# Two-layer decoder kernel: the first layer's scatters issued one step later, and its last group's router weights computed earlier

## The reference, cut to what matters

```python
x = x + linear_attention(norm(x))            # first layer
x = x + cross_attention(norm(x), ctx_1024)   # 16 heads, softmax over 77 keys
x = x + experts(norm(x))                     # 16 experts, two per token, capacity 640
x = x + latent_attention(norm(x))            # second layer
x = x + cross_attention_1head(norm(x), ctx_1024)
x = x + quantised_ffn(norm(x))
```

```python
top_vals, sel = top_k(sigmoid(xf @ gate_w.T), 2)
weights = top_vals / (top_vals.sum(-1, keepdims=True) + 1e-06)
slot = where(rank < 640, expert * 640 + rank, none)   # rank: place of the token in its expert's queue
padded[slot] = x                                      # each token is written to two slots
out = (expert_output[slot] * weights).sum(axis=1)
```

## Time and profile before

| | us |
|---|---|
| median of 3 runs | 1657.05 |
| lowest and highest of them | 1647.87, 1658.19 |
| the profiled execution, its own time | 1666.73 |
| its span in the trace | 1664.7 |

### The profile page before, as it was taken

How to read it: one execution, slowest core, us unless ns; L and a number is a source line. 1 busy time by engine, 2 the same in 40 slices (tenths; PEclk the granted TensorE clock), 3 DMA queues, 4 the chain that set the end, 5 groups by cost and what they waited for, 6 DMA issues and landing times. The chain is left out here.

```text
span 1664.7 us, 26844 instructions
## 1 busy us (share of the span) xinstructions
PE 1514.0 (91%) x9735; PEld 1071.9 (64%) x9735; DVE 1014.5 (61%) x2312; ACT 900.2 (54%) x2289; POOL 473.1 (28%) x625
## 2 busy tenths in 40 slices
PE   8999999898977889999999899999999989996299
PEld 5766777676656767787777566666666654442288
DVE  3657878888886335222222566766664568777883
ACT  4457786675786222211212555666656633597980
POOL 3212334344345300000002665555533300032100
PEclk9999999999997899999999999999999979998599
DMA  4441111111241144333424211110100000000031
GB/s 120 153 160 25 39 38 40 37 51 51 82 133 45 58 154 136 123 114 125 152 90 137 71 39 52 41 35 28 39 14 14 1 26 1 0 0 18 21 101 64
DMA packets 105281, 109.33 MB, mean 66 GB/s; under 512 B 29762, under 2 KB 94156, under 8 KB 105152
## 3 DMA queue, kind: packets, MB, share of 16 engines
q1 hardware_dynamic: 99008, 91.06, 17.8%
q0 software_dynamic: 6144, 16.57, 3.1%
HBM read 65.81 MB, written 42.01 MB: 65 GB/s over the span
## 5 line engine op out<-in xcount | busy, mean ns | idle before, releaser
L2121 ACT ACTIVATE c_pr<-bank,c_nmax 128x256 f32<-128x256 f32 x256 | 117.7, 472 | 118.0 <-DVE c_nmax L2238 117.9
L1827 POOL TENSOR_SCALAR c_pr<-c_pr,c_rsum 128x256 f32<-128x256 f32 x256 | 127.6, 514 | 186.4 <-DVE c_rsum L2243 186.0
L1558 ACT ACTIVATE b_G<-bank 128x320 f32<-128x320 f32 x128 | 55.9, 437 | 210.4 <-PE bank L1507 210.4
L1507 PE MATMUL bank<-b_XT,shared 128*128 128x320 f32 x512 | 154.2, 436 | 0.0
L2238 DVE TENSOR_REDUCE c_nmax<-bank 128x2 f32<-128x512 f32 x128 | 82.4, 686 | 105.8 <-PE bank L1886 102.5
L1521 PE MATMUL bank<-shared,b_G 128*128 128x256 f32 x640 | 142.2, 379 | 0.0
L959 ACT ACTIVATE a_L<-a_L,a_Lm 128x77 f32<-128x77 f32 x512 | 131.2, 353 | 4.4 <-DVE a_Lm L1097 4.3
L1521 PEld LDWEIGHTS bank<-shared,b_G 128*128 128x128 f32 x640 | 120.9, 190 | 17.8
L508 POOL TENSOR_TENSOR a_Pm<-a_L,a_xrden 128x1024 f32<-128x1024 f32 x32 | 61.3, 1916 | 220.6 <-DVE a_xrden L1104 220.6
L1507 PEld LDWEIGHTS bank<-b_XT,shared 128*128 128x128 f32 x512 | 92.2, 192 | 27.4 <-issue 1.0
L1577 DVE COPY b_Y<-bank 128x256 f32<-128x256 f32 x80 | 34.0, 425 | 119.8 <-PE bank L1521 119.6
(11 more groups left out here) (386 smaller groups left out, 3433.1 us busy)
## 6 DMA issues: line engine op xcount, KB each, us to landing
shared<-L_ffn_w SPq DMA_DIRECT2D x32, 512.0 KB, 6.1
t_slots_in<-a_h SPq DMA_DIRECT2D x20, 512.0 KB, 6.2
shared<-t_slots_in SPq DMA_DIRECT2D x15, 640.0 KB, 7.0
t_slots_out<-b_Y SPq DMA_DIRECT2D x15, 640.0 KB, 4.1
hT_all<-x SPq DMA_DIRECT2D x8, 512.0 KB, 3.8
a_xr<-x SPq DMA_DIRECT2D x8, 512.0 KB, 3.9
t_x_a<-a_x SPq DMA_DIRECT2D x8, 512.0 KB, 2.9
shared<-t_x_a SPq DMA_DIRECT2D x8, 512.0 KB
```

What stands on the lines that cost most here:

```text
L1507: t = p.matmul(P[2 + n % 2][:, 0:HC], w1[e % 3][:, u, 128 * f:128 * f + 128], XT[e % 2][:, u, HC * m:HC * m + HC], start=(u == 0), stop=(u ...
L1827: p.tensor_scalar(pr[k][:, e, u, :], pr[k][:, e, u, :], rsum[k][:, e, u:u + 1], 1.0, ALU.mult, ALU.mult).then_inc(q.pr_ready, 1)
L2121: a.activation(pr[t % 2][:, e, u, :], P[e][:, S * u:S * u + S], ACT.Exp, bias=nmax[t % 2][:, e, u:u + 1], accum_out=sums[t % 2][:, e, u:u ...
```

## The change

Three edits. First, GpSimd issues `scatter(g - 5, 0)` in step 1, behind `normalised(g - 3, 3)`, and `scatter(g - 5, 1)` in step 2, ahead of `one_of_two`; before it was step 0 and step 1. Second, the loop has one step more, so that the last group's second half still has its step. Third, VectorE computes `weigh` of the last group (7) in step 7 of round 11, directly behind `place_tokens` and ahead of the three L1309 of that step, instead of in step 1 of round 12. For the groups 0 to 6 `weigh` stays where it was.

```diff
-        FIRST, LAST = -2 * NS + 2, (NG + 4) * NS + 2
+        FIRST, LAST = -2 * NS + 2, (NG + 4) * NS + 3
...
-                    if s in (0, 1) and there(g - 5):
-                        scatter(g - 5, s)
+                    if s in (1, 2) and there(g - 5):
+                        scatter(g - 5, s - 1)
...
-                    if s == 1 and there(g - 5):
+                    if s == 1 and there(g - 5) and g - 5 < NG - 1:
                         weigh(g - 5)
...
                         if back4:
                             place_tokens(g - 4)
+                            if g - 4 == NG - 1:
+                                weigh(g - 4)
```

## The result

The changed kernel takes 1660.44 us (median of 12 runs, 1655.72 to 1664.96). The kernel before, run beside it, takes 1656.33 (12 runs, 1647.87 to 1659.18). The ratio is 1.0035, with a 95% interval of 1.0023 to 1.0048. That is 5.8 us slower by the ratio (the medians differ by 4.1): within 1% and inside my range, but on the other side of the forecast, and the interval excludes "no change".

A forecast was written before the change was run, and what follows sets the result against it. Between 500 and 550 us no engine was taken as full; a chain of waits through VectorE, GpSimd and TensorE bound the kernel. 0 + 2.0 - 3.5 = -1.5 us against the median 1657.05 gave 1655.5 us, range 1647 to 1663.

The forecast's parts named there:

- I enter nothing for rounds 5 to 7: Rounds 5 to 7: GpSimd's later work finds slack while linear attention fills TensorE; 0, or 0.6 us in all without cover.
- The rule: Shared SBUF port: GpSimd's products hold VectorE's L1221 in round 10, up to 2.4 us of VectorE's time; entered as nothing.
- Rounds 8 to 10, +2.0: Rows of eight scatters delay products by 3.0, then 5.8 us; round 10's removed 3.85 us wait leaves 2.0 us late.
- The 0.8 us that I took from round 9's divisor: Round 9: a free GpSimd starts the products 0.1 us behind the divisor, so 0.8 us is to be had.
- Carrying the 2.0 to the end: From round 10's products on, TensorE and the last routers follow each other, so +2.0 us reaches the layer's end.
- The hand-over, -3.5: Last group's weights early: the barrier before the experts moves from 594.82 to 591.35, -3.5 us, with TensorE's idle transposes last.
- The landing of 3.0 us from issue: Hand-over: the last scatter, generated by 585.19, lands at 587.2, taking 3.0 us as the second layer's gathers; loads issued by 589.5.
- The clock behind the barrier, 0 with -2.0 as the bound: Experts' first matmuls: with 1.2 us idle the clock may not have fallen; entered 0, at most -2.0 us.
- The delay stays whole: Round 10's 3.85 us do not come back and round 9's 5.8 us reach the end: +2.3, 1659.4 us; chance 0.15.
- The port rule costs in full: Round 10: VectorE's hold delays the addition behind `weigh` and TensorE's bank by 2.4 us: +0.9, 1658.0 us; chance 0.08.
- The hand-over gains nothing: Before the experts, SyncE's wait for scatters or its own stores ends as late as before: +2.0, 1659.0 us; chance 0.12.
- Stalls that go with the scatters: Round 8: VectorE's unexplained 3.07 us wait is caused by step 0's transfers and goes with them: -4.6, 1652.5 us; chance 0.15.

The follow-up runs named there:

- second trace of before: The unedited kernel before, traced again with the follow-up experiments: an execution of 1652.39 us; its timed runs gave 1653.09 us, ratio 1.0000.
- the best version: Kernel before with the last group's weights early and the scatters in steps 1 and 2 from round 10 on only: 1646.89 us, 0.9967; repeated, 1646.51 us, 0.9949.
- scatter edits alone: Kernel before with only the first two edits, scatters in steps 1 and 2, the last group's weights where they were: 1661.12 us, ratio 1.0038.
- Rounds 8 and 9 alone: Kernel before with the scatters in steps 1 and 2 in rounds 8 and 9 only: 1658.44 us, ratio 1.0040.
- The first trace: The trace of the unedited kernel before that the prediction priced from: an execution of 1666.73 us, slower than any other run of that kernel.
- `a_rstd` first: Changed kernel with the second half of each scatter in step 3 behind L488 instead of in step 2: 1654.66 us, ratio 1.0010 against the kernel before.
- `weigh` alone: Kernel before with only the third edit, the last group's router weights behind its slot numbers: 1652.52 us, ratio 0.9981.
- the two second traces: Repeat traces of both unedited kernels: the changed kernel's execution of 1660.93 us and the kernel before's of 1652.39 us; the repeated timing gave ratio 1.0040.

## Why the prediction was wrong, step by step

- **The step that failed: "I enter nothing for rounds 5 to 7, and 0.2 us of each, 0.6 us in all, if that cover is gone."** The runs have +3.8 for round 5 and about +2 for round 7. I had also taken TensorE to be filled by the next linear attention there; in the second trace of before it idled 1.32 us for VectorE in round 5. I asked only when `a_rstd` and the products would come. L488 was to end at 302.6, and the trace has 302.61; but VectorE was ready at 301.6 and stood 1.02 us for it, not 0.2. And I did not ask what would then stand beside L1146. Before, GpSimd idled 3.06 us between L488 and L508. The delay used up that gap, so L508 follows L488 at once, and the end of L488 lets L1146 start on VectorE as well. L508 starts 0.04 us earlier and L1146 lasts as long as L508.
- **The rule was weighed in the wrong place.** I had the trace's own example, L1221 held for 2.59 us beside L508, and priced it for round 10 alone. There the hold came (1.72 us), and the stretch from 9 to 10, shortened by the full 3.9 us in the best version, shows that it costs nothing there. The Trainium skill (SBUF — State Buffer, "Who interferes with whom") says that whichever of the two starts first keeps the port to its end. That holds for L1146 as well, which reads two SBUF inputs, and the trace of round 5 agrees with 1.88 against 0.15 us.
- **How 1.7 us became 3.8.** With the 0.5 us that the late `a_rstd` adds, the hold of 1.7 delays VectorE by 2.2 us, and TensorE waits 2.2 us longer. Then it works at the lower clock level for 3.4 us, which costs 1.7. The two sum to 3.9 us. In "scatter edits alone" it works there for 6.8 us, and the round costs 5.7.
- **Round 7.** Its 2.3 us are 0.9 of the row of eight and TensorE's longer time at the lower clock (0.93 instead of 0.97). That the round pays by itself is shown by the traces of the kernels with it alone, though not by their times; what keeps the clock down for longer is not.
- **Rounds 8 to 10, +2.0: right in size, and in its mechanism but for one term.** From round 8's mark to round 10's it is 78.4 and 78.5 us in the changed kernel and 76.4 in the second trace of before. Rounds 8 and 9 alone cost 7.7 us there; round 10's wait gives most of it back. The 0.8 us that I took from round 9's divisor don't hold, so that the sum came out is in part luck: in the second trace of before GpSimd waits 0.40 us for that divisor, so nothing is to be had there. That the mark of round 9 moved by 1.9 and not by 3.0 has another reason, as far as the windows show: in the changed kernel the clock is 0.56 over the 4.0 us from 471.13, in which TensorE is busy for 0.93 us only, while in the second trace of before it is low where TensorE works (0.62 over the 4.0 us from 464.55, all of them busy). With rounds 8 and 9 alone the mark moves by 3.2.
- **Carrying the 2.0 to the end: too much.** Between round 10's mark and the last scatter the changed kernel needs 43.8 us, the second trace of before 45.7. So 1.9 us were taken up on the way. "Scatter edits alone" has 1.7 of them, so they don't come from `weigh`. TensorE's next transposes and the window of the 8.0 us behind the mark, first in the second trace of before, then in the changed kernel:

```profile
531.43 1.97 PE L705 MATMUL bank<-ident,a_Pm 128*128 128x128 f32 x8 [6.10 <-POOL a_Pl L509]
...
529.00:537.00 8.00, 5.57 (x29) 5.56 (x30) 0.00 (x0) 2.66 (x5) 6.32 (x6) 0.57 0.19 68
```

```profile
540.01 1.09 PE L705 MATMUL bank<-ident,a_Pm 128*128 128x128 f32 x8 [0.19 <-POOL a_Pl L509]
...
537.50:545.50 8.00, 7.44 (x56) 6.33 (x58) 3.89 (x9) 5.41 (x13) 6.58 (x7) 1.00 0.16 51
```

Before, TensorE stands 6.10 us for `a_Pl` and then works at a clock of 0.57; in the changed kernel L705 waits 0.19 us, and the clock stays up. L705 starts 2.48 us behind the mark in both, and VectorE's next L1309 (L1311) 12.61 us behind it before and 11.06 in the changed kernel: 1.55 of the 1.9 us. So the wait that the change removes in round 10 is worth more than its 3.85 us, and this was no term of my sum.
- **The hand-over, -3.5: mis-sized, and its order wrong.** Measured is -2.1, and SyncE's loads are last, not TensorE. I had read 7.4 us between the last scatter's end and the loads; in the second trace of before it is 3.4 (575.61 to 578.99). The first trace is 7.2 us longer from round 10 to the experts, with a wait of 4.01 us in it that came from no engine of the core, and the 11.82 us from its last scatter to the transposes stand alone beside the 7.68 to 8.14 of the six other traces without the third edit. So the row that I priced from was stretched by chance. The landing of 3.0 us from issue was too long as well: the loads are issued 2.33 us after the last scatter's start. For that the Trainium skill (DMA: Bandwidth & Descriptors, "Anatomy of one DMA — SWDGE (gpsimd) path") has about 2.0 us of fixed cost, and the trace agrees with at most 2.33.
- **The clock behind the barrier, 0 with -2.0 as the bound: wrong sign in this kernel.** The idle time fell from 4.70 to 2.29 us, but the clock spent the same 6.8 us at its lower level, and more of it fell on the first matmuls (4.47 instead of 3.12 us). I had reckoned that a shorter wait leaves the clock up. In no run here does it stay up behind this wait, but in "`a_rstd` first", with 2.33 us of idle time, it is down for 3.4 us only, and the way from the first transposes to the second eight matmuls is 0.6 us shorter than before instead of 1.3 longer. What decides between the two I can't say.
- **The rivals.** "The delay stays whole" falls, since the 3.85 us came back. "The port rule costs in full" names the right mechanism at the wrong instruction. "The hand-over gains nothing" falls, with `weigh` alone at 0.9981. "Stalls that go with the scatters" falls: those waits are in one trace of the thirteen only, and the second trace of the same kernel has none.

In one line: forecast 0 + 2.0 - 3.5 = -1.5; measured, by stretches of the two second traces, 7.1 (of which 1.0 is chance) + 2.1 - 1.9 - 2.1 + 1.2 = +6.4 us, against 6.6 by the ratio.

## What to carry to other kernels

When a change makes one engine late, don't stop at whether its results are still in time: list what the other engines run at the instants at which it now starts, above all where the end of one instruction lets one on GpSimd and one with two SBUF inputs on VectorE start together. An edit inside a loop has a price in every round, and each stage has its own; here the same edit shortens the way to round 10's products by 3.9 us and costs 3.8 in round 5, and making it conditional on the round turned 5.8 us lost into 5.5 to 8.4 won. Before pricing a wait, take a second trace if there is one, or at least look for waits that no engine of the core ended.

## What the runs showed of the hardware

- A SCALAR_TENSOR_TENSOR of VectorE on 128x4 elements took 0.15 us where it began ahead of GpSimd's next product or at the end of one, and 1.88 us when it began 0.04 us behind a TENSOR_TENSOR of GpSimd on 128x1024. That is seen in four traces, and not in the one in which four transfers were put between.
- `weigh`'s L1221, a TENSOR_TENSOR on 128x4 elements, took 1.71 to 1.73 us beside GpSimd's L508 in rounds 5 to 9 of ten traces, and 2.59 or 2.60 in round 9 of the other three. It was the products and not the indirect transfers that held it: in round 10 it took 0.16 us with GpSimd in its row of transfers and 1.72 us beside L508.
- Executions of the same program differ by waits of 3 to 4 us that end with nothing on the core, three of them in one trace of before and none in the twelve other traces.
- A wait of TensorE had a price beyond its length where the clock fell to its lower level behind it: 1.7 us in round 5, behind a wait that had grown by 2.2 us, and about 1.5 us in round 10, behind 6.10 us.
- The clock behind a wait of the same length differs between executions: behind 2.29 us of idle time at the hand-over it was 0.61 over 3.0 us and 0.50 over the next 4.5, behind 2.33 us in another kernel 0.52 over 3.0 us and 0.90 over the next 2.7.
